# Copying the final gate and up weights to DRAM earlier, deeper buffering of the row loads, and a new order on VectorE in tiles 13 to 15

## The reference

```python
def ternary_quant(w):                       # groups of 64, bf16
    scale = clip(mean(abs(w_g)), 1e-8)
    q = clip(round(w_g / scale), -1, 1)
    return w + (q * scale - w)
def ffn(x):                                 # hidden 2048
    gate, up = split(x @ ternary_quant(w_gate_up).T)
    return rms_norm(silu(gate) * up) @ ternary_quant(w_down).T
def attn(x):                                # 16 heads of 32, linear attention
    q, k, v = relu(q), relu(k), [v, 1]
    vk = v @ k.T; out = vk @ q
    return (out[:-1] / (out[-1] + 1e-15)) @ w_proj.T + b_proj
x = x + 0.5 * ffn(layernorm(x))
x = x + attn(layernorm(x))
x = x + 0.5 * ffn(layernorm(x))
```

## Time and profile before

| what | us |
|---|---|
| median of 3 runs | 865.76 |
| lowest and highest run | 863.02, 870.5 |
| the profiled execution, its own time | 867.0 |
| its span, from first to last instruction | 865.1 |
| TensorE busy | 843.8 (98%) |
| VectorE busy | 597.4 (69%) |
| ScalarE busy | 479.6 (55%) |
| GpSimd busy | 74.6 (9%) |
| mean granted TensorE clock | 0.996 of full |

### The profile page before, as it was taken

The page is one execution under the profiler, slowest core; times in us unless marked ns, Lnnn a source line. Parts: engine busy times, 40 slices in busy tenths (PEclk is TensorE's granted clock), DMA queues, the critical chain, the costliest instruction groups (busy, mean ns, idle before and its releaser), DMA issues. The chain is left out here.

```text
span 865.1 us, 13381 instructions
## 1 busy us (share of the span) xinstructions
PE 843.8 (98%) x4877; PEld 405.3 (47%) x4942; DVE 597.4 (69%) x1120; ACT 479.6 (55%) x902; POOL 74.6 (9%) x123
## 2 busy tenths in 40 slices
PE   6999999999999999899999999999999999999998
PEld 5644444444444444364646464444444444444445
DVE  7999997924597666575787868576667666764451
ACT  7986667536654455564666545355545454544460
POOL 2211001201011010000101011000000000000000
PEclk9999999999999999999999999999999999999999
DMA  9999408995868879771223135432543424343346
GB/s 258 187 171 137 78 1 167 215 226 165 181 198 208 164 156 201 158 132 22 56 32 65 23 102 222 137 71 45 110 88 69 95 62 94 62 95 68 84 81 146
DMA packets 264240, 104.48 MB, mean 121 GB/s; under 512 B 248560, under 2 KB 251376, under 8 KB 262128
## 3 DMA queue, kind: packets, MB, share of 16 engines
q1 hardware_dynamic: 254048, 74.80, 45.1%
q0 software_dynamic: 6176, 21.50, 9.0%
q10 hardware_dynamic: 3952, 7.34, 2.7%
HBM read 33.82 MB, written 12.58 MB: 54 GB/s over the span
## 5 line engine op out<-in xcount | busy, mean ns | idle before, releaser
L2013 PE MATMUL proj_ps<-down_w,slots 128*128 128x512 bf16 x502 | 111.4, 379 | 0.6 <-issue 0.2
L1410 DVE SCALAR_TENSOR_TENSOR slots<-slots,inv 128x512 f16<-128x512 f32 x124 | 90.7, 743 | 5.8 <-ACT slots L974 5.6
L974 ACT ACTIVATE slots<-slots,inv 128x512 f16<-128x512 f32 x124 | 86.0, 711 | 13.5 <-POOL inv L826 8.9
L1397 DVE SCALAR_TENSOR_TENSOR slots<-up_ps,silu 128x512 f32<-128x512 f32 x61 | 42.0, 688 | 64.7 <-ACT silu L953 40.8
L1994 PE MATMUL gate_ps<-gu_w,xT 128*128 128x512 bf16 (+1 forms) x386 | 81.8, 353 | 2.7 <-ACT silu L953 2.3
L1994 PE MATMUL up_ps<-gu_w,xT 128*128 128x512 bf16 (+1 forms) x382 | 81.4, 352 | 1.1 <-DVE slots L1397 0.6
L2013 PEld LDWEIGHTS proj_ps<-down_w,slots 128*128 128x128 f16 x512 | 49.9, 98 | 60.9 <-DVE xs L1419 0.8
L963 ACT ACTIVATE o_buf<-slots 128x512 f32<-128x512 f32 x72 | 45.2, 628 | 51.4 <-DVE slots L1397 50.8
L821 POOL TENSOR_TENSOR few<-few 128x1 f32<-128x1 f32 x48 | 32.4, 674 | 282.4 <-DVE few L1367 274.9
L2013 PE MATMUL gate_ps<-down_w,slots 128*128 128x512 bf16 x250 | 55.9, 379 | 0.3
L1994 PEld LDWEIGHTS gate_ps<-gu_w,xT 128*128 128x128 f16 x392 | 35.9, 98 | 42.8 <-ACT silu L953 3.9
(11 more groups left out here) (277 smaller groups left out, 1562.3 us busy)
## 6 DMA issues: line engine op xcount, KB each, us to landing
gu_kept<-gu_w POOLq DMA_DIRECT2D x4, 1024.0 KB, 4.7
gu_forms_kept<-att_w POOLq DMA_DIRECT2D x4, 1024.0 KB, 6.6
gu_w<-gu_kept POOLq DMA_DIRECT2D x4, 1024.0 KB, 6.3
att_w<-gu_forms_kept POOLq DMA_DIRECT2D x4, 1024.0 KB, 12.1
out_dram<-xs SPq DMA_DIRECT2D x15, 256.0 KB, 2.0
xs<-in_L_attn_x_dram SPq DMA_DIRECT2D x3, 1024.0 KB, 8.9
aw<-in_L_attn_w_qkv_dram ACTq DMA_DIRECT2D x12, 256.0 KB, 2.9
slots<-in_L_ffn_w_gate_up_dram ACTq DMA_DIRECT2D x5, 512.0 KB, 6.9
```

The lines of the kernel that those rows point to most:

```text
L974: nc.scalar.activation(h_halves(i)[:, 0, q * 512:(q + 1) * 512], h_rows(i, q), ACT.Copy, scale=inv[:, i % 8:i % 8 + 1]).then_inc(hi_done, 1)
L1397: nc.vector.scalar_tensor_tensor(out=h_rows(i, q), in0=bank(up_ps, j), scalar=gu_out(i), in1=silu_rows(j), op0=ALU.mult, op1=ALU.mult).the ...
L1410: nc.vector.scalar_tensor_tensor(out=h_halves(i)[:, 1, q * 512:(q + 1) * 512], in0=h_rows(i, q), scalar=inv[:, i % 8:i % 8 + 1], in1=h_hal ...
L2013: mm = nc.tensor.matmul(proj_bank(i), h_turned(i)[:, r, j, :], down_w[:, j, :], start=(r + j == 0), stop=(r == 1 and j == HC - 1))
```

## The change

It does three things.
- `keep_weights` is called on GpSimd right after the last `load_piece`, four times in a row ahead of `inverse(0)`, and each copy waits for its own quarter's weights (`wq_done` at 4, 8, 12, 16), not for all 24 pieces. The calls in tiles 8 to 11 go.
- The rows for row sums go into four buffers (the third is the bias's, which holds rows of the last piece before; the fourth the end of `x_buf`), three ahead; ScalarE issues four loads at the start where it issued two. `weight_parts`, which writes two of these buffers, waits for all row sums.
- On VectorE, `ln_stats(4, 3)` and `mean_squares(13)` come ahead of `pair_low(3)` in (13, 3), `turn_shift` of tiles 1 and 3 moves from (14, 0) to (13, 3), and `forms_sums(4, 1)` from (14, 2) to (15, 0).

The semaphore for turned pairs is split by parity, and a table `PAIR_SLOT` names the slots that the pairs have already.

```diff
+PAIR_SLOT = (6, 6, 7, 7, 7, 7)
+def same_slot_before(n):
+    return max(k for k in range(n) if PAIR_SLOT[k] == PAIR_SLOT[n])
+        unit_rows = (aw_raw[:, 0, :], aw_raw[:, 1, :], aw[:, 3 * D:4 * D], x_buf[:, 6 * D:7 * D])
             def keep_weights(q):
-                pool.wait_ge(wq_done, PIECES)
+                pool.wait_ge(wq_done, 4 * q + 4)
                 nc.gpsimd.dma_start(gu_kept[:, q, :], gu_w[:, q, :, :, :].rearrange("p s k f -> p (s k f)"))\
                   .then_inc(gu_saved, 16)
+            for q in range(QH):
+                keep_weights(q)
             for i in range(EARLY):
                 inverse(i)
...
             for i in range(EARLY, LAYER):
                 if i < 12:
                     rstd(3, i % TILES)
-                    keep_weights(i % TILES)
...
+            def load_rows(u):
+                nc.scalar.dma_start(unit_rows[u % 4], qkv_v[u] if u < 12 else proj_v[u - 12]).then_inc(unit_here[u % 4], 16)
+            for p in (20, 21, 23):
+                act.wait_ge(wt_here[p % 3], 16 * ((p - PE_TURNED) // 3 + 1))
+            for u in range(4):
+                load_rows(u)
...
             def row_sum(u):
-                act.wait_ge(aw_here[u % 2], 16 * (u // 2 + 1))
-                if 0 < u < UNITS - 1:
-                    load_unit(u + 1)
+                act.wait_ge(unit_here[u % 4], 16 * (u // 4 + 1))
                 if u:
                     act.wait_ge(abs_done, u)
+                    if u + 3 < UNITS:
+                        load_rows(u + 3)
...
             def weight_parts(n):
                 act.wait_ge(powers_done, 1)
+                act.wait_ge(abs_done, UNITS)
...
+                if (i, q) == (13, 3):
+                    ln_stats(4, 3)
+                    mean_squares(13)
                 for n in pairs_cut(i)[q // 2:q // 2 + 1]:
                     if q % 2:
                         pair_low(n)
...
-                if (i, q) in ((12, 3), (14, 0)):
+                if (i, q) in ((12, 3), (13, 3)):
                     for t in (0, 2) if i == 12 else (1, 3):
                         turn_shift(4, t)
-                if (i, q) in ((13, 1), (14, 2)):
-                    forms_sums(4, i - 13)
+                if (i, q) in ((13, 1), (15, 0)):
+                    forms_sums(4, (i - 13) // 2)
...
-                mean_squares(i)
+                if i != 13:
+                    mean_squares(i)
```

More of the change, by code:

```diff
@@ L394, in w_cut @@
         def w_cut(n):
-            return slot(6 if n < 2 else 7).bitcast(F16)[:, 0:2 * WIDE].rearrange("p (r n) -> p r n", r=2)
+            return slot(PAIR_SLOT[n]).bitcast(F16)[:, 0:2 * WIDE].rearrange("p (r n) -> p r n", r=2)
         def pair_raw(n):
@@ L483, in macaron_kernel @@
         aw_here = [sem(f"aw_here{i}") for i in range(2)]
+        unit_here = [sem(f"unit_here{i}") for i in range(4)]
         raw_here = [sem(f"raw_here{i}") for i in range(2)]
-        pairT_here = sem("pairT_here")
+        pairT_here = [sem(f"pairT_here{i}") for i in range(2)]
         projT_here = [sem(f"projT_here{i}") for i in range(2)]
@@ L704, in turn_pair @@
                     sp.dma_start_transpose(place.rearrange("p o k m -> p (o k) m"), w_cut(n)[:, r, :])\
-                      .then_inc(pairT_here, 16)
+                      .then_inc(pairT_here[n % 2], 16)
             def load_unit(u):
@@ L849, in _, with keep_weights @@
                 load_piece(p)
+            def keep_weights(q):
+                pool.wait_ge(wq_done, 4 * q + 4)
+                nc.gpsimd.dma_start(gu_kept[:, q, :], gu_w[:, q, :, :, :].rearrange("p s k f -> p (s k f)"))\
+                  .then_inc(gu_saved, 16)
+            for q in range(QH):
+                keep_weights(q)
             for i in range(EARLY):
@@ L1079, in unit_high @@
             def unit_high(u):
-                act.wait_ge(aw_here[u % 2], 16 * (UNITS // 2 + (u - 12) // 2 + 1))
+                act.wait_ge(aw_here[u % 2], 16 * ((u - 12) // 2 + 1))
                 if u >= 14:
@@ L1093, in pair_high @@
                 else:
-                    act.wait_ge(pairT_here, 32 * n)
+                    k = same_slot_before(n)
+                    act.wait_ge(pairT_here[k % 2], 32 * (k // 2 + 1))
                 for rows, cols in ((pair_raw(n)[:, HALF:], slice(0, 3 * HALF)), (w_sums, slice(3 * HALF, WIDE))):
@@ L1117, in forms_high @@
                 nc.scalar.activation(x_cut[:, 0, cols], x_forms[:, cols], ACT.Copy).then_inc(xhigh_done, 1)
[L1119 to L1123, removed]
             def row_sum(u):
-                act.wait_ge(aw_here[u % 2], 16 * (u // 2 + 1))
-                if 0 < u < UNITS - 1:
-                    load_unit(u + 1)
+                act.wait_ge(unit_here[u % 4], 16 * (u // 4 + 1))
                 if u:
                     act.wait_ge(abs_done, u)
-                nc.scalar.activation(aw_hl[:, 1, :], aw_raw[:, u % 2, :], ACT.Abs, accum_out=rowsum[:, u:u + 1])\
+                    if u + 3 < UNITS:
+                        load_rows(u + 3)
+                nc.scalar.activation(aw_hl[:, 1, :], unit_rows[u % 4], ACT.Abs, accum_out=rowsum[:, u:u + 1])\
                   .then_inc(abs_done, 1)
@@ L1395, in hidden @@
                 if i in (14, 15) and q == 0:
-                    dve.wait_ge(pairT_here, 64 if i == 14 else 32 * WEIGHT_PAIRS)
+                    for k in range(2):
+                        dve.wait_ge(pairT_here[k], 32 if i == 14 else 96)
                 nc.vector.scalar_tensor_tensor(out=h_rows(i, q), in0=bank(up_ps, j), scalar=gu_out(i),
@@ L1744, in attention_ahead @@
                         pair_sums(n)
-                if (i, q) in ((12, 1), (12, 2), (13, 2), (13, 3)):
-                    ln_stats(4, {(12, 1): 0, (12, 2): 2, (13, 2): 1, (13, 3): 3}[i, q])
-                if (i, q) in ((12, 3), (14, 0)):
+                if (i, q) in ((12, 1), (12, 2), (13, 2)):
+                    ln_stats(4, {(12, 1): 0, (12, 2): 2, (13, 2): 1}[i, q])
+                if (i, q) in ((12, 3), (13, 3)):
                     for t in (0, 2) if i == 12 else (1, 3):
                         turn_shift(4, t)
-                if (i, q) in ((13, 1), (14, 2)):
-                    forms_sums(4, i - 13)
+                if (i, q) in ((13, 1), (15, 0)):
+                    forms_sums(4, (i - 13) // 2)
                 if (i, q) in ((13, 3), (15, 3)):
@@ L2119, in product @@
                     pe.wait_ge(formT_here[s], 32 * (b + 1))
-                    pe.wait_ge(pairT_here, 32 * DC)
+                    for k in range(2):
+                        pe.wait_ge(pairT_here[k], 16 * DC)
                 elif p == 1:
-                    pe.wait_ge(pairT_here, 32 * WEIGHT_PAIRS)
+                    for k in range(2):
+                        pe.wait_ge(pairT_here[k], 16 * WEIGHT_PAIRS)
                 if p in (1, 2, 7):
```

3 lines of the change are left out of this document (removed).

## The result

| what | before | after |
|---|---|---|
| median of 6 runs of each, us | 864.83 | 878.4 |
| lowest and highest run | 863.02, 870.5 | 876.45, 880.49 |
| the profiled execution and its span | 867.0, 865.1 | 879.36, 877.5 |
| mean granted TensorE clock | 0.996 | 0.990 |

The ratio is 1.0148, 95% interval 1.0118 to 1.0178. The direction was right; the size was not. 871.5 was forecast, and 878.4 lies above the range.

The account below looks back on a forecast made before the run. The prediction took TensorE, busy 843.8 of 865.1 us, as the bound. Stall 4.6, clock 1.7, row loads -0.3 and VectorE's order -0.3 sum to +5.7 us, giving 871.5 from the median 865.76; range 862 to 877.

Parts of the forecast that it names:

- What bounds the kernel: Whole kernel: TensorE is busy 843.8 of 865.1 us, so other engines can only give back its idle time, 6.8 us.
- In turn, the copies end first ... the four take 10.9 us: First stage: piece 20's transposing DMA waits out four copies at 2.6 us a MB, lands at 103.2; TensorE stalls 4.6 us.
- with 32 x 0.02 us for the small packets between: First stage, beside the copies: piece 20's small packets, taken in turn, add only 32 x 0.02 us.
- By 92 us it has 665 packets left: First stage: piece 20's transposing DMA still has 665 packets, 0.16 MB, to move at 92 us, needing 1.5 us.
- the copies go at half pace: Rival for the early copies: DRAM writes under load stall TensorE 17 us, clock 1.7 more, 883.9 us in all; chance 8%.
- Pieces 21 to 23 ... add nothing: First stage, behind piece 20: these follow within 1.5 us each and are taken 4 us apart, so no further stall.
- The clock: TensorE behind the first-stage stall: the granted clock falls, as after the earlier 2.16 us wait, costing 1.74 us.
- The copies' old place, "worth 0": Tiles 8 to 11: losing four copies gains 0, since nothing on TensorE's path waited for a DMA there.
- The row loads, "cost 0, at most 1 if the turned tile 2 came late": ScalarE at 143 to 148 us: two more starting loads cost 0, at most 1; a tile 8 wait gives -0.3 us.
- VectorE's order: Tiles 14 and 15: TensorE's 1.85 us wait goes, the 0.60 ahead of 341.13 becomes about 2.1; net -0.3 us.
- From there all follows `hidden(15, 0)` as before, the 2.16 at 362 too: After tile 15's wait: the later timeline keeps its place behind `hidden(15, 0)`, and the sixth attention product's 2.16 us wait stays.
- The saturated engines: From 328 to 341 us: DMA engines are full (109.7%), so pair 5 lands by bytes; `hidden(15, 0)` gains only 0.3 us.

Follow-up runs that it names:

- experiment 6: The kernel before with all four copies early, each cut in four DMAs of smaller packets: 865.9 us, ratio 1.0003.
- experiment 4: The changed kernel with its four copies held back until piece 23 is turned: 865.85 us, ratio 0.9995 to the kernel before.
- experiment 11: The kernel before, own copies kept, plus eight unused 1 MB DRAM-to-DRAM copies, four at the early place, four once piece 23 is turned: 873.89 us, ratio 1.0076.
- experiment 9: The changed kernel with copies after piece 23's turning, two row loads later, and pair 3's second turning ahead of pair 5's loads: 860.53 us, ratio 0.9944.
- experiment 10: The kernel of experiment 9 with the copies left in tiles 8 to 11, as before the change: 860.54 us, ratio 0.9943.
- experiment 8: The kernel before with the change's VectorE order, and pair 3's second turning issued on SP ahead of pair 5's loads: 863.51 us, ratio 0.9992.
- experiment 3: The kernel before with the change's VectorE order alone: 864.52 us, ratio 0.9989.
- experiment 1: The kernel before with the four early copies alone, row loads and VectorE's order as before: 878.12 us, ratio 1.0154.
- experiment 5: The kernel before with the copies of quarters 0 and 1 early, the other two left in tiles 10 and 11: 874.8 us, ratio 1.0108.
- experiment 7: The changed kernel with copies after piece 23's turning, and two row loads at the start, the next two one tile-step later each: 863.6 us, ratio 0.9981.

## Why the prediction was wrong, point by point

- **What bounds the kernel:** right. TensorE's idle time was the account in which every gain and loss turned up.
- **"In turn, the copies end first ... the four take 10.9 us":** here it failed. That piece 20 waits for the copies was right, the engine, the line and the landing's cause too. The term mis-sized is the copies' pace: from 92 us, where the sum begins, to 110.2 is 18.2 us for 4.19 MB, 4.3 us a MB in place of 2.6 (some of the copies' packets had passed before 92, so the pace behind it was slower still). Piece 20 landed at 110.4 in place of 103.2, and the stall was 12.7 in place of 4.6. With pace 4.3 the sum's own working gives 92 + 18.2 + 1.05 - 98.34 - 1.28 = 11.6; most of the rest is the 0.9 us by which the stage ran earlier in the execution after.
- **"with 32 x 0.02 us for the small packets between":** right for 98 to 101 us of the changed kernel (95 packets of each kind, the small ones 3.6% of the engines' time), wrong behind it. At 104 to 110 us 692 small packets passed beside 138 of q0 and took 79.7% of the engines' time, 0.11 us each. The sum had no term for that.
- **"By 92 us it has 665 packets left":** wrong, though the sum doesn't hang on it, since by its rule the copies end first either way. Between 90 and 92 us q1 moved one packet in the changed kernel (experiment 6), so piece 20 had nearly all of its 1024 before it.
- **Why I took the wrong pace:** The earlier trace rows show copies from DRAM back into the on-chip memory; the ones moved go the other way. Direction alone isn't it: in experiment 4 the moved copies, with nothing beside them, go at 2.6 us a MB too. What slows them is the transposing neighbour, more so with the source on the chip (experiment 11). The only row of copies in that direction beside a transposing DMA was the earlier trace rows, at 6 us a MB, and the prediction had even written "though these come from DRAM" beside the faster one. It was kept as a bound and a rival of 8%, "the copies go at half pace", 883.9. The truth lay between the two, nearer to that rival. Experiment 11 shows that a source in DRAM gives back most of the pace.
- **"Pieces 21 to 23 ... add nothing":** right, no further gap.
- **The clock:** 1.7 was added behind the stall; the two groups there cost 0.4 + 1.0 = 1.4. Right within 0.3.
- **The copies' old place, "worth 0":** right, experiments 9 and 10 have medians 0.01 us apart.
- **The row loads, "cost 0, at most 1 if the turned tile 2 came late":** the mechanism named is the one that came; it cost 1.66 us in the changed kernel, 0.8 alone, 1.4 in experiment 4. The -0.3 of tile 8 was right for the profiled execution and too small for others: with two buffers the same wait was 0.9, 2.1 and 3.1 us in the profiles of experiments 11, 8 and 3 (none in those of 1, 5 and 6), and of the executions with four buffers that were profiled none has it. That the spread of the runs stems from it fits experiments 7, 9 and 10, but no run took it alone.
- **VectorE's order:** tile 14's wait gone and a longer one ahead of (15, 2), as forecast ("about 2.1", measured 2.8), and ScalarE did wait for pair 3, 3.2 us. **"From there all follows `hidden(15, 0)` as before, the 2.16 at 362 too"** failed: the clock now fell behind tile 15's gap (2.87 + 2.64 - 2 x 1.89 = 1.7 us), TensorE came later to the sixth product by that, and the wait there was gone together with the fall of the clock behind it (1.74). The late stages gave back 2.4 us, not 0.3.
- **The saturated engines:** "if pair 5 lands more than a microsecond sooner ..., the reading was wrong". It didn't in the changed kernel: from the first step of `pair_high(3)` to `hidden(15, 0)` are 31.7 us there, 31.5 before. Experiment 8 made `hidden(15, 0)` 3.2 us sooner by an earlier issue, so full engines weren't its limit.

Not settled: what the packets share when both streams read from the on-chip memory, and why the small ones take 0.11 to 0.22 us in the later part where they took 0.02. Experiments 1, 5 and 11 show how the stall goes with amount and source, experiment 6 changed packet size and moment together; where in the path it arises, no run shows.

## What to carry to other kernels

Before a large copy is moved to where "the queue is empty", look at what the other queues have to land there, and size it by a row of the same direction with the same neighbour; here a pace from the opposite direction, with nothing beside it, was 1.7 times too fast. If a DMA with small packets stands on the path, hold the copies back until it has landed; that took the whole loss away. To cut each copy in four DMAs did so too, but the piece that it saved had a head start, and the next one still landed with the last copy. And when a wait is removed, follow the DMA that it uncovers: the row loads and VectorE's order measured nothing alone, and 0.57% together once two issues were put in another place (two loads later, one turning ahead of loads).

## What the runs showed of the hardware

- Four copies of 1 MB with 8 KB packets from the on-chip memory to DRAM land 2.7 us apart with nothing beside them (experiment 4), 4.4 in the changed kernel and 6.0 in experiment 1 beside transposing DMAs. From DRAM to DRAM they land 3.0 apart beside them (experiment 11). In experiment 1, at 104 to 112 us, the small packets too take longer: 523 of 0.25 KB take 88.5% of 16 engines for 8 us, 0.22 us each.

```profile
q1 hardware_dynamic: 523, 0.13, 88.5%
q0 software_dynamic: 164, 1.19, 36.0%
```

- The Trainium skill (DMA: Bandwidth & Descriptors, Queues, rings and completion order) states the round-robin between queues by packets. The traces agree at 98 to 101 us of experiment 1 and 94 to 100 us of experiment 11 (101 against 104, 301 against 300), by the packets that the trace counts. They don't show it at 98 to 106 us of experiment 5 (81 against 1024). Nor does the order give the price: a pair of packets comes every 16/34 = 0.47 us on an engine with the copies' source on chip and every 16/50 = 0.32 with it in DRAM. In the first stretch the packets' own time is only 71.2% + 6.5% of the engines', so part of the 0.47 is time between packets.
- Piece 21's turning, 0.26 MB, held SP for 12.8 us of issue, where piece 20's took 1.3 (1.2 before the change): what SP had to issue next was late as well.
